# Attention 0 of a gated two-layer block: residual, norm and transposes batch by batch inside the loop, first FFN units prepared beside the last heads

## What is computed

```python
x = x + tanh(g_xattn[0]) * L0_xattn(layernorm(x), ctx, ctx, mask)   # 16 heads of 32
x = x + tanh(g_ffn[0])   * L0_ffn(layernorm(x))   # silu(x w1) * (x w2) -> gelu h1 -> gelu h2 -> w3
x = x + tanh(g_xattn[1]) * L1_xattn(layernorm(x), ctx, ctx)          # with output projection
x = x + tanh(g_ffn[1])   * L1_ffn(layernorm(x))   # quantized gate, up and down
```

## Time and profile before

| | |
|---|---|
| three runs | 1711.61, 1713.25, 1715.65 us, median 1713.25 |
| the profiled execution | 1712.6 us, of which the span from first to last instruction 1710.5 |
| granted clock, mean | 0.975 |
| PE busy | 1597.7 us, 93% |
| weight loads (PEld) | 1446.6 us, 85% |
| DVE, ACT, POOL busy | 1110.3, 968.2, 255.4 us |
| chain that ended last | PE 82%, DVE 6%, ACT 4%, issue 4%, DMA 2%, POOL 1% |

### The profile page before, as it was taken

One profiled execution on the slowest core, in us unless ns is written; L12 is line 12 of the kernel. 1 busy time (PEld: TensorE's weight loads), 2 busy tenths in 40 slices (PEclk: granted clock), 3 DMA queues, 4 the chain that ended last, 5 costly groups with the idle time before them and its releaser, 6 DMA issues.

```text
span 1710.5 us, 25606 instructions
## 1 busy us (share of the span) xinstructions
PE 1597.7 (93%) x9264; PEld 1446.6 (85%) x9264; DVE 1110.3 (65%) x1967; ACT 968.2 (57%) x2020; POOL 255.4 (15%) x328
## 2 busy tenths in 40 slices
PE   5899999999972999999999998989999999999898
PEld 5799999989962999999899996777999899998655
DVE  6377777777786465333565545464777777778786
ACT  4376777666661355444444434335676677767575
POOL 2012111111100000000010000101121202113651
PEclk9999999999985999999999999999999999999999
DMA  6566766676633223554355553346666676658400
GB/s 202 135 167 150 196 171 177 154 185 164 152 105 131 95 96 129 183 185 163 115 173 201 207 179 107 118 127 144 182 166 171 165 191 162 177 134 201 163 12 28
DMA packets 147113, 259.38 MB, mean 152 GB/s; under 512 B 40997, under 2 KB 90277, under 8 KB 146849
## 3 DMA queue, kind: packets, MB, share of 16 engines
q1 hardware_dynamic: 146528, 257.43, 53.3%
q10 hardware_dynamic: 448, 0.14, 0.0%
HBM read 189.10 MB, written 58.57 MB: 145 GB/s over the span
## 4 chain that ended last, share of the span: by engine, by line
PE 82%; DVE 6%; ACT 4%; issue 4%; DMA 2%; POOL 1%; SPq 0%; ACTq 0%; DVEq 0%; POOLq 0%
PE ps L923 27%; PE ps L647 16%; PE ps L643 14%; PE ps L688 7%; PE ps L700 7%; PE ps L675 2%; PE ps L678 2%; PE ps L730 2%; PE ps L853 1%; PE ps L866 1%; DVE wl_f L1411 1%; ACT P L1522 1%; PE ps L677 1%; PE ps L676 1%; PE ps L625 1%
## 5 line engine op out<-in xcount | busy, mean ns | idle before, releaser
L923 PE MATMUL ps<-ah_f,wh_f 128*128 128x400 f32 x1280 | 443.8, 347 | 14.9 <-POOL low_f L1961 8.3
L923 PE MATMUL ps<-al_f,wh_f 128*128 128x400 f32 x1280 | 442.2, 345 | 0.0
L923 PEld LDWEIGHTS ps<-ah_f,wh_f 128*128 128x128 f32 x1280 | 242.0, 189 | 18.0 <-issue 10.5
L1060 DVE TENSOR_REDUCE nmax<-ps 100x1 f32<-100x722 f32 x256 | 220.9, 904 | 45.5 <-PE ps L677 42.7
L923 PEld LDWEIGHTS ps<-al_f,wh_f 128*128 128x128 f32 x1280 | 242.2, 189 | 0.1
L1522 ACT ACTIVATE P<-ps,nmax 100x722 f32<-100x722 f32 x256 | 219.9, 861 | 20.7 <-DVE nmax L1060 20.4
L1834 POOL TENSOR_TENSOR cxl<-raw,cxh 128x384 fp32r<-128x384 f32 (+1 forms) x120 | 118.7, 1011 | 670.3 <-ACT cxh L1487 663.4
L1531 ACT ACTIVATE PT<-ps 128x400 fp32r<-128x400 f32 x384 | 166.9, 505 | 84.5 <-PE ps L688 83.3
L1066 DVE TENSOR_TENSOR PT<-ps,PT 128x400 fp32r<-128x400 f32 x384 | 197.0, 568 | 3.8
L643 PE MATMUL ps<-cxh,wkh 128*128 128x338 f32 (+1 forms) x512 | 173.4, 339 | 21.9 <-DVE wkl L1039 12.7
L1407 DVE CAST wh_f<-raw_f 128x1024 fp32r<-128x1024 f32 x88 | 60.9, 692 | 181.6 <-PE ps L923 160.2
(11 more groups left out here) (172 smaller groups left out, 2585.3 us busy)
## 6 DMA issues: line engine op xcount, KB each, us to landing
KS<-kd SPq DMA_DIRECT2D x192, 361.0 KB
raw_f<-in_h SPq DMA_DIRECT2D x64, 512.0 KB, 4.8
raw_f<-in_gud SPq DMA_DIRECT2D x48, 512.0 KB, 5.6
raw<-in_ctx SPq DMA_DIRECT2D x64, 192.0 KB, 3.8
kd<-ksh SPq DMA_DIRECT2D x64, 192.0 KB, 2.1
kd<-ksl SPq DMA_DIRECT2D x64, 192.0 KB, 2.3
raw_f<-in_w SPq DMA_DIRECT2D x24, 512.0 KB, 3.6
raw<-in_ctx SPq DMA_DIRECT2D x64, 169.0 KB, 4.5
```

The source lines that it names most:

```text
L923: return e.matmul(o, p, q, start=start, stop=stop)
L1060: e.tensor_reduce(m.nmax[0:S, c:c + 1], scores_of(n), AX.X, ALU.max, negate=True).then_inc(v_max, 1)
```

## The change

1. **Residual in the loop.** At i % 8 == 5 (from 13 on) PE turns the finished attention output of the batch before back (`turn_out`, four transposes into one ring bank), DVE adds it to x in one buffer x0 for all batches (`add_out`) and takes the statistics (`stats_out`). SP loads x0 at step 3 and stores it at step 6 of a batch.
2. **Norm and transposes in the loop.** POOL computes the inverse root of a batch (`batch_root`, eight small instructions, step 6), DVE norms x0 (`normal_out`, at i % 8 == 0), PE transposes it at i % 8 == 1 (`turn_normal`, four transposes into a ring bank). For batches 0 to 5 ACT keeps the result in the room of the used-up queries (`keep_normal`), and POOL splits it into `act` at steps 57 to 62 (`split_kept`). Batch 6 (`KEPT`) is normed at step 62 and transposed at step 63, batch 7 after the loop; both are split by ACT and DVE. Batch 7's bias moves from ACT to DVE (`add_last_bias`).
3. **First units ready early.** SP fetches units 0 to 3 at step 57. POOL, not DVE, rounds and subtracts units 0 to 2 (`prepare`, steps 58 and 60, unit 2 after the loop); ACT measures them at steps 62, 63 and after (`measure_low`) and loads the SiLU table at 62. For this attention 0 lies differently in SBUF (`PLACE`).
4. **Column parts.** Units 0 and 1 are issued in parts of the 800 columns (`inputs`), between the last transposes.
5. The re-load of all batches before the FFN is gone, and semaphore counts follow.

The ring gains an item ("res") at each `turn_out` and one ("xn") at each `turn_normal`:

```diff
+KEPT = 6
+def turned_at(i):
+    if i == NP - 1:
+        return KEPT
+    return i // 8 - 2 if i % 8 == 1 and 16 < i < NP else None
...
         RINGS[_l] += beside(_i)
+        if _l == 0 and 8 < _i < NP and _i % 8 == 5:
+            RINGS[_l].append(("res", _i // 8 - 1))
+        if _l == 0 and turned_at(_i) is not None:
+            RINGS[_l].append(("xn", turned_at(_i)))
...
+RINGS[0] += [("res", B - 1), ("xn", B - 1)]
```

SP, within the loop:

```diff
+                    if L == 0 and p == 3 and b:
+                        load_x0(b - 1)
+                    if L == 0 and p == 6 and b:
+                        store_x0(b - 1)
...
+                    if L == 0 and i == 57:
+                        w.wait_ge(p_job, NJOB)
+                        w.wait_ge(p_pv, 56)
+                        w.wait_ge(g_cx, 60)
+                        for u in range(4):
+                            fetch(("unit", u))
```

PE:

```diff
+                def turn_out(b):
+                    if b < B - 1:
+                        w.wait_ge(a_fin, 4 * b + 4)
+                    else:
+                        w.wait_ge(v_bias, 4)
+                    ring_free(("res", b))
+                    for g in range(4):
+                        ins = e.transpose(ps[0:S, ring_bank(L, ("res", b)), 128 * g:128 * g + 128],
+                                          m.QT[:, g, S * b:S * b + S], ident[:, :])
+                    ins.then_inc(p_res, 1)
...
                     for j in beside(i):
                         job(j)
+                    if L == 0 and i > 8 and i % 8 == 5:
+                        turn_out(i // 8 - 1)
+                    if L == 0 and turned_at(i) is not None:
+                        turn_normal(turned_at(i))
                     if L and i in OUT_AT:
                         project(OUT_AT[i])
                     if i:
                         weigh(i - 1)
                 if L == 0:
                     weigh(NP - 1)
                     turn_sums(B - 1)
+                    inputs(0, 0, HN, 0, g_xf, 4)
+                    turn_out(B - 1)
+                    inputs(1, 0, HN, 0, g_xf, 4)
+                    inputs(0, HN, HN + 3 * S, 0, v_xf, 1)
+                    turn_normal(B - 1)
+                    inputs(0, HN + 3 * S, N, 1, v_xf, 2)
+                    inputs(1, HN, N, 1, v_xf, 2)
                     return
```

ACT and DVE, within the loop:

```diff
+                    if L == 0 and i < NP - 1 and turned_at(i) is not None:
+                        keep_normal(turned_at(i))
...
+                    if L == 0 and i in (62, 63):
+                        measure_low(i - 62)
+                    if L == 0 and i == 62:
+                        e.activation(warm[:, :], ident[:, 0:1], ACT.Silu)
...
+                    if L == 0 and i == NP - 1:
+                        low_normal(KEPT)
                     for j in beside(i):
                         low_job(j)
+                    if L == 0 and 8 < i < NP and i % 8 == 5:
+                        add_out(i // 8 - 1)
+                        stats_out(i // 8 - 1)
+                    if L == 0 and 8 < i < NP and i % 8 == 0:
+                        normal_out(i // 8 - 2)
+                    if L == 0 and i == NP - 2:
+                        normal_out(KEPT)
```

POOL:

```diff
+                def prepare(u):
+                    z, r = u % 4, FETCHED["unit", u] % 4
+                    w.wait_ge(d_raw[r], raw_done(("unit", u)))
+                    me.then(e.tensor_copy(wh[:, z, :], raw[:, r, :]))
+                    me.settle()
+                    e.tensor_tensor(wl[:, z, :], raw[:, r, :], raw32(wh[:, z, :]), ALU.subtract).then_inc(g_ul, 1)
...
+                    if L == 0 and (8 < i < 56 and p == 6 or i == 61):
+                        batch_root(b - 1)
+                    if L == 0 and i in (58, 60):
+                        prepare((i - 58) // 2)
+                    if L == 0 and 57 <= i < 63:
+                        split_kept(i - 57)
...
                 spread_sums(B - 1)
                 if L == 0:
+                    spread_low(0)
+                    spread_low(1)
+                    prepare(2)
+                    batch_root(B - 1)
+                    spread_low(2)
                     return
```

More of the change, by code:

```diff
@@ new lines, in flamingo_kernel @@
+            m.nmax = at(f"nmax_{L}", o["nmax"], [128, 4])
+            m.wk = [at(f"wk{c}_{L}", o["wk"] + 8192 * i, [128, 4, D], F32R) for i, c in enumerate("hl")]
+            V = [at(f"V{z}_{L}", o[f"V{z}"], [128, KT * 2 * D], F32R) for z in range(2)]
+            m.QS = at(f"QS_{L}", o["QS"], [98, 2, H, S], F32R)
+            PT = at(f"PT_{L}", o["PT"], [128, 2 * 2 * KT * 2 * S], F32R)
+            m.sum = at(f"sum_{L}", o["sum"], [128, 2 * S])
+            m.KS = at(f"KS_{L}", o["KS"], [98, 2, 4, T], F32R)
@@ L497, in attention, with load_x0, store_x0, fetch @@
                             load_ctx(L, m, b + 2, p // 4, k)
+            def load_x0(b):
+                if b:
+                    w.wait_ge(p_xf, b)
+                e.dma_start(x0, t["x"][b]).then_inc(d_x[0], 16)
+            def store_x0(b):
+                w.wait_ge(v_x0, b + 1)
+                e.dma_start(X[0][b], x0).then_inc(d_xo[b], 16)
+            def fetch(item):
+                r = FETCHED[item]
+                if r >= 4:
+                    w.wait_ge(a_raw, FREE_AT[FETCH[r - 4]] + 1)
+                ap = weight(item[1]) if item[0] == "unit" else block_of(item[1])
+                e.dma_start(raw[:, r % 4, :], ap).then_inc(d_raw[r % 4], 16)
             def load_w(L, m, i):
@@ L582, in store @@
                 e.dma_start(wqd[i // 2, :, 1024 * (i % 2):1024 * (i % 2) + 1024], qst[i % 2]).then_inc(d_wq[i % 2], 16)
-            for u in range(4):
-                fetch(("unit", u))
             kept = []
@@ L599, in _ @@
             w.wait_ge(v_hid, len(HID))
+            for b in range(B):
+                w.wait_ge(d_xo[b], 16)
             e.dma_start(s3, t["s3"].partition_broadcast(S)).then_inc(d_s3, 16)
@@ L712, in turn_sums, with turn_normal @@
                     ins.then_inc(p_inv, 1)
+                def turn_out(b):
[8 more added lines that the diff above has]
+                    ins.then_inc(p_res, 1)
+                def turn_normal(b):
+                    w.wait_ge(v_xn, 8 + b + 1)
+                    ring_free(("xn", b))
+                    for k in range(4):
+                        ins = e.transpose(ps[:, ring_bank(L, ("xn", b)), S * k:S * k + S], x0[:, 128 * k:128 * k + 128],
+                                          ident[0:S, 0:S])
+                    ins.then_inc(p_xf, 1)
                 def turn_x(b):
@@ L974, in _ @@
                                                    u == 80 and kk == 0, u == 87 and kk == 1) for b in range(B)])
-                             for kk in range(2)])
+                             for kk in range(2)]).then_inc(p_u, 1)
             attention(1)
@@ L1411, in prepare @@
                 e.tensor_tensor(wl[:, z, :], raw[:, r, :], raw32(wh[:, z, :]), ALU.subtract).then_inc(v_ul, 1)
-            for u in range(3):
-                prepare(u)
             for u in range(UNITS):
@@ L1753, in attention, with measure_low @@
                     turn_h(n, q)
-            attention(0)
-            w.wait_ge(v_x0, B)
-            for b in range(B):
-                w.wait_ge(d_xo[b], 16)
-            for b0 in (0, 4):
-                root(b0, 4)
-                for b in range(b0, b0 + 4):
-                    turned(b, p_xf, b + 1, act[0][:, 0:4, S * b:S * b + S], a_xf)
-            def prepare(u):
+            def measure_low(u):
                 z, r = u % 4, FETCHED["unit", u] % 4
-                w.wait_ge(v_ul, u + 1)
+                if u < 3:
+                    w.wait_ge(g_ul, u + 1)
+                else:
+                    w.wait_ge(v_ul, u - 2)
                 if u >= 4:
@@ L1770, in prepare @@
                 e.activation(raw[:, r, :], raw32(wl[:, z, :]), ACT.Abs, accum_out=low[:, z, 0:1]).then_inc(a_raw, 1)
-            for u in range(3):
-                prepare(u)
+            attention(0)
             for u in range(UNITS):
@@ L1951, in attention, with spread_low @@
                 quantize(4)
-                roots(3)
+                tile_roots(3)
                 quantize(5)
                 quantize(6)
-            attention(0)
-            for u in range(UNITS):
+            def spread_low(u):
                 w.wait_ge(a_raw, FREE_AT["unit", u] + 1)
@@ L1961, in _ @@
                 e.partition_all_reduce(low[:, u % 4, 1:2], low[:, u % 4, 0:1], 128, MAXR).then_inc(g_low, 1)
+            attention(0)
+            for u in range(UNITS):
+                if u >= 3:
+                    spread_low(u)
                 if u == 43:
```

231 lines of the change are left out of this document (141 added, 90 removed).

## The result

| | before | after |
|---|---|---|
| median (13 runs each) | 1713.25 us | 1707.88 us (1704.65 to 1710.38) |
| profiled execution | 1712.6 us | 1707.16 us, span 1705.4 |
| granted clock, mean | 0.975 | 0.979 |
| PE, DVE, ACT, POOL busy | 1597.7, 1110.3, 968.2, 255.4 us | 1606.4, 1100.6, 964.7, 290.9 us |

The ratio of the runs is 0.9968, interval 0.9959 to 0.9976: 5.4 us faster, 4 to 7 by the interval.

The account below looks back on a forecast made before the run. PE was taken to bound the loop, with a hole around 510 to 555 us. Gaining 23.0 us in the hole (tail included) and losing 16.2 in the loop takes 6.8 off 1712.6: 1706 us, range 1691 to 1717.

Parts of the forecast that it names:

- The loop, 16.2 us: Steps 13 to 56: eleven added transpose groups make PE wait for ring banks, 6 x 1.40 + 5 x 1.56 us lost.
- That PE's clock would fall in the loop: Rival, loop: each of eleven new waits is followed by half clock, 50 us more, 1756 us; chance 0.13.
- That the ring waits could be hidden (0.12): Rival, loop: only 4.2 us of transposes stay, 12 us less, 1694 us; chance 0.12.
- The tail, 3.5 us plus 0.6: Steps 57 to 63: 0.8 us of weigh waits, 2.7 for ACT's measurement and table; DVE's batch 6 transposes 0.6 more.
- the table's term: Step 62: ACT's measurement of unit 0 and SiLU table load make the last transposed weights' copies 2.7 us later.
- POOL late for batch 6's sums (0.15): Rival, tail: GpSimd copies batch 6's sums late, holding DVE's queue; 2 to 5 us, 1709 us; chance 0.15.
- The code loads, 7 us each: GpSimd after the loop: each switch between all-reduce and two-input arithmetic costs 7 us; three switches, two ahead of the mark.
- That the loads cost nothing (0.10): Rival, after the loop: GpSimd's code loads are free, gain 21 us, 1691 us; chance 0.10.
- The chain from the copy to the mark, 32.8 us: After the loop: from GpSimd's copy of the last sums (513.1) through loads, all-reduces, root and products to 545.9 us.
- the mark: End of unit 1's FFN products, behind which nothing changes: about 568.9 us before, forecast 545.9 without the loop's loss.
- The sum: Whole kernel: 23.0 us gained in the hole, tail included, 16.2 lost in the loop, so 6.8 gained: 1706 us.
- the signs named ahead: Loop steps 1.4 to 1.6 us longer, three GpSimd pauses and PE idle about 7 us, first FFN product at 538.

Follow-up runs that it names:

- Experiments 5: The change with its added transposes ahead of the step's K and V jobs, weighed pair ahead of maxima, DVE's residual and ACT's norm copy early: 1702.00 us, ratio 0.9928.
- 9: Experiments 5 and 6 together, but in batch 7 DVE takes the maxima ahead of the weighed pair again: 1691.37 us, ratio 0.9867.
- 12: Experiment 9 with, in the residual's steps, DVE's residual between the two maxima and the first K job's copies first on ACT and DVE: 1689.56 us, ratio 0.9857.
- experiments 2: The change with unit 2's weights prepared by GpSimd at step 62 instead of after the loop: 1702.23 us, ratio 0.9930.
- 4: The change with ACT's measurement of unit 0 and the SiLU table load moved from step 62 to behind step 63's copies: 1708.79 us, ratio 0.9969.
- 8: The change with one tiny multiplication put between GpSimd's first two all-reduces: 1723.16 us, ratio 1.0049.
- Experiments 3: The change with DVE's last reciprocal ahead of its step 63 parts of the transposed weights: 1705.98 us, ratio 0.9949.
- experiment 6: The change with the tail reordered: unit 2 split at step 60, all-reduces grouped, table load behind ACT's last copy, last reciprocal earlier: 1699.64 us, ratio 0.9914.

## Why the prediction came out right, step by step

- **The loop, 16.2 us.** 17.3 measured, by the same eleven waits. The handoffs were exact (1.40 and 1.57 us), the restart of the weigh, 0.1 us each, was missing. Experiments 5, 9 and 12 show it from the other side: with the order changed and the same work left in, the price falls to 8.3 and then 5.0 us. That PE's clock would fall in the loop did not happen in these steps: it is 1.00 over the whole stretch from 130 to 480 us. The Trainium skill (TensorE: Matmul & The Clock Gate, HAM oscillation) describes such falls for pauses of several microseconds; waits of 0.8 to 1.1 us, as here, do not bring them. At or just behind step 57, where PE waits 1.6 to 2.2 us, the clock falls in nine of the thirteen profiles with the change and stays up in four. So this rival (0.13) had a place, in the tail, and its price there was small.
- **That the ring waits could be hidden (0.12).** Not as the change is written, but experiment 12 nearly does it.
- **The tail, 3.5 us plus 0.6.** 3.8 measured at the copy of the last sums. Its parts: 2.2 us at steps 57 and 58 instead of 0.8, where the wait itself is worth 0.7 (experiments 2, 4, 8 and 12) and PE's fallen clock the other 1.5. Most of this is given back where the clock was up earlier than before (the last exps are only 0.8 us late by 525.5, start and loop taken off). ACT's measurement and table cost 2.2 us instead of 2.7. Experiments 3 and 4 show that the table's term does not stand by itself: in both profiles the last reciprocal comes under 2 us earlier, since it has two conditions, and with both taken away (experiment 6) the copy comes 3.5 us earlier.
- **POOL late for batch 6's sums (0.15).** It waited 0.66 us for DVE there and was not late. The CAST of 1024 columns takes 1.04 to 1.10 us, less than the 1.2 taken; the splits fit.
- **The code loads, 7 us each.** 5.78 and 6.80 us on the path, against 7 taken for each: the row that I took, 6.96 us, was of the second kind. Of the three two bind: PE's first product waits for the first, the norm of batch 7 for the second. Experiment 8 prices one more pair at 15.6 us, more than the 14 of two such rows. The Trainium skill (GPSIMD Engine Reference, 2.1 Instruction dispatch) has about 6 us for the first call of freshly loaded code, with no instruction to be seen; the loads ahead of an all-reduce agree (5.6 to 6.2 us, once 8.17), those ahead of arithmetic are longer (6.8 to 7.7 where nothing was waited for). The change-over at the program's start, which fitted into 4.95 us of idle time before, fits into 4.71 in after; no run tells why it is shorter. That the loads cost nothing (0.10) is refuted by experiment 8.
- **The chain from the copy to the mark, 32.8 us.** 30.6 measured: the loads 1.4 us shorter, the first two all-reduces 0.7 us instead of 2.0, the rounding and the subtraction 0.6 us shorter together, and PE's products of batch 7's columns 7.9 us instead of 6.7, as the clock was at 0.50 through most of them. PE's waits, foreseen as 7 us, were 4.36 and 2.90.
- **The sum.** At the mark 6.8 us forecast, 6.6 measured, 8.2 without the late start; at the end 5.4. So the mechanism was right in its main terms, but the agreement of 1706 and 1707.9 to 2 us is in part luck. It rests on errors of 1 to 2 us that offset each other: loop 1.1 too small, hole 2.2 too large, and the clock at the program's start and behind unit 15 not foreseen at all. Of the signs named ahead, the FFN's first product came where it was said (538.6 for 538), and the steps with the norm are 1.7 us longer, a little over the 1.4 to 1.6 said.

## What to carry to other kernels

An item put into a ring of two buffers costs not its own length but the release of the item before it; place it where the item before was emptied long ago, and give whoever empties the new one that job first, ahead of its long work. On GpSimd count the switches between the all-reduce and TENSOR_TENSOR or TENSOR_SCALAR arithmetic and pay 6 to 8 us for each (a CAST behind an all-reduce paid none); group the all-reduces, and do the arithmetic in the loop. When moving one wait gains less than it should, look for the second condition in the same in-order queue before dropping the cause, and measure both removed together.

## What the runs showed beyond that

DVE's norm of 100 x 512 in place takes 0.54 us, but up to 0.98 when POOL's subtraction is running as it starts. DVE at step 56 of after, with POOL's row, and the same instruction in experiment 6 with POOL idle:

```profile
495.30 0.97 DVE L1241 TENSOR_SCALAR x<-x,mv,rq 100x512 f32<-100x512 f32 x1
```

```profile
494.94 1.05 POOL L2037 TENSOR_TENSOR al_f<-QT,ah_f 128x400 fp32r<-128x400 f32 x1
```

```profile
525.92 0.54 DVE L1241 TENSOR_SCALAR x<-x,mv,rq 100x512 f32<-100x512 f32 x1
```

The Trainium skill (SBUF — State Buffer, Who interferes with whom) has the two engines share one pair of ports that one of them holds for a whole instruction; the traces agree closely. In every profile with the change, a norm that started while POOL's subtraction was running ended 0.28 or 0.29 us after that subtraction, whether it then took 0.67, 0.86 or 0.97 us. A CAST of POOL that began during the norm did not lengthen it.

A pause of PE can be paid twice. In after, 4.7 us of it ahead of batch 7's columns were followed by 1.2 GHz; in experiment 2, 2.1 us of it were followed at first by the full clock, and the 3.0 us by which the root came earlier became 4.5 at u2. How long a pause may be is not shown: a wait of 1.6 us at step 57 was followed by the low clock in some profiles and not in others.
